# Routed experts of a one-core audio tower: groups of 384 rows in place of groups of 512

## What is computed

```python
h = _L0_tok_ref(x)                                  # 512 x 512 self attention over the channels of each batch
h = h + _L0_attn_ref(_layernorm(h), Wq, Wk, Wv, Wo) # 8 heads, 2 kv heads, 125 tokens a batch
h = h + _L0_ffn_ref(_layernorm(h), gate_w, w1, w2, w3, sw1, sw2, sw3, expert_bias)
```

```python
scores = softmax(xf @ gate_w)
_, sel = top_k(scores + expert_bias[None, :], 2)
routed_in = xf[token_idx] * top_scores_sorted[:, None]          # sorted by expert, 32000 rows of 512
h = silu(ragged_dot(routed_in, w1, counts)) * ragged_dot(routed_in, w3, counts)   # 512 -> 448
routed_out = ragged_dot(h, w2, counts)                          # 448 -> 512
out = (silu(xf @ sw1) * (xf @ sw3) @ sw2).at[token_idx].add(routed_out)
```

## Time and profile before

| | |
|---|---|
| median of 3 runs | 5948.72 us (5947.63 to 5953.92) |
| the profiled execution's own time | 5945.65 us |
| its span, first to last instruction | 5943.9 us |
| PE busy | 5809.3 us, 98% of the span |
| weight loads (PEld) busy | 4785.6 us, 81% |
| DVE busy | 4301.6 us, 72% |
| ACT busy | 2970.2 us, 50% |
| POOL busy | 2043.9 us, 34% |
| mean granted TensorE clock | 0.991 of 2.4 GHz |

### The profile page before, as it was taken

How to read it: one execution, slowest core, us unless ns; L and a number is a source line. 1 busy time by engine, 2 the same in 40 slices (tenths; PEclk the granted TensorE clock), 3 DMA queues, 4 the chain that set the end, 5 groups by cost and what they waited for, 6 DMA issues and landing times. The chain is left out here.

```text
span 5943.9 us, 103011 instructions
## 1 busy us (share of the span) xinstructions
PE 5809.3 (98%) x30600; PEld 4785.6 (81%) x30600; DVE 4301.6 (72%) x9758; ACT 2970.2 (50%) x5510; POOL 2043.9 (34%) x1725
## 2 busy tenths in 40 slices
PE   5999999999999999999999996999999999999999
PEld 4888888888888888888888885788888888888887
DVE  4888888888888888888888885666666666666665
ACT  3555555555555555555555553444444444444443
POOL 1333333333333333333333332333333333333332
PEclk8999999999999999999999998999999999999999
DMA  2111111111111111111111111666666556666641
GB/s 73 47 49 43 46 49 43 45 49 44 45 50 44 44 49 45 44 49 45 43 49 46 43 48 47 161 156 162 157 156 158 153 153 158 162 157 154 159 125 46
DMA packets 317180, 504.89 MB, mean 85 GB/s; under 512 B 78676, under 2 KB 151380, under 8 KB 317012
## 3 DMA queue, kind: packets, MB, share of 16 engines
q1 hardware_dynamic: 246228, 372.69, 20.8%
q0 software_dynamic: 70912, 131.71, 11.3%
HBM read 379.43 MB, written 140.28 MB: 87 GB/s over the span
## 5 line engine op out<-in xcount | busy, mean ns | idle before, releaser
L1428 POOL DMA_INDIRECT out_dram<-res,goal x280 | 530.6, 1895 | 1121.8 <-DMA out_dram<-res,goal 687.1
L930 POOL TENSOR_SCALAR ve<-ag 125x1 f32<-125x1 f32 x256 | 56.1, 219 | 1618.7 <-DVE ag L755 942.6
L639 ACT ACTIVATE e<-ps,negmax 128x512 f32<-128x512 f32 x512 | 349.2, 686 | 513.2 <-PE ps L449 408.0
L1172 PE MATMUL ps<-rT_hi,up_hi 128*128 128x512 f32 x1960 | 536.7, 395 | 1.6 <-DVE rT_lo L1336 1.6
L1172 PE MATMUL ps<-rT_lo,up_hi 128*128 128x512 f32 x1960 | 536.8, 395 | 0.0
L1172 PE MATMUL ps<-rT_hi,up_lo 128*128 128x512 f32 x1960 | 536.4, 395 | 0.0
L1264 ACT ACTIVATE uT_hi<-egb 128x512 fp32r<-128x512 f32 (+1 forms) x280 | 177.1, 632 | 540.4 <-DVE egb L1355 540.4
L1172 PEld LDWEIGHTS ps<-rT_hi,up_hi 128*128 128x128 f32 x1960 | 369.1, 188 | 89.9 <-issue 2.0
L1172 PEld LDWEIGHTS ps<-rT_lo,up_hi 128*128 128x128 f32 x1960 | 369.1, 188 | 88.0
L1172 PEld LDWEIGHTS ps<-rT_hi,up_lo 128*128 128x128 f32 x1960 | 368.9, 188 | 88.0
L942 POOL TENSOR_TENSOR qk_low<-X,qk_high 125x1024 fp32r<-125x1024 f32 x128 | 305.9, 2390 | 343.0 <-ACT qk_high L626 343.0
(11 more groups left out here) (216 smaller groups left out, 15487.4 us busy)
## 6 DMA issues: line engine op xcount, KB each, us to landing
raw<-in_L_ffn_w SPq DMA_DIRECT2D x140, 768.0 KB, 5.1
X<-in_x SPq DMA_DIRECT2D x128, 750.0 KB
raw<-in_L_ffn_w SPq DMA_DIRECT2D x70, 896.0 KB, 4.8
normed_rows<-y SPq DMA_DIRECT2D x128, 250.0 KB
out_dram<-h SPq DMA_DIRECT2D x128, 250.0 KB
raw<-in_L_ffn_w SPq DMA_DIRECT2D x210, 128.0 KB, 6.2
rows<-normed_rows,entries POOLq DMA_INDIRECT x280, 4.1
out_dram<-res,goal POOLq DMA_INDIRECT x280, 5.2
```

The costliest lines, as they stand in the source:

```text
L639: nc.scalar.activation(e[:, i, :], ps[:, (i + 1) % 2, :], ACT.Exp, bias=negmax[:, i:i + 1], accum_out=total[:, i:i + 1]).then_inc(e_sb.sem, 1)
L1172: ins = nc.tensor.matmul(ps[:, bank, :], w[a][:, k, col:col + P], rT[b][:, k, :], start=(k == 0 and i == 0), stop=(k == KC - 1 and i == 2))
L1428: nc.gpsimd.indirect_dma_start(out, bass.IndirectOffsetOnAxis(ap=goal[group[1] % 2][:, i:i + 1], axis=0), res[i][:], None, bounds_check=la ...
```

## The change

The number of tiles in a group goes from 4 to 3, and what follows from that: 91 groups (an odd number, so `each_group` has one more static call), planning that divides by three (five more small DVE operations), PSUM tiles cut to 384 columns in the up projection and the gate, signals of inner blocks counted by four (`block_of`) while those of tiles count by three, and waits for the tile that last used a bank (`LAST_IN_BANK`), since banks 0 and 1, and 6 and 7, no longer alternate evenly over groups. The four inner blocks of a group, its weights and their loads stay as they are.

```diff
-GROUP_TILES = 4
+GROUP_TILES = 3
...
     NG = (2 * TOKENS - E) // GROUP + E
-    NG += NG % 2
+    assert NG % 2 == 1
...
-                    then(nc.vector.tensor_scalar(groups[:], groups[:], float(GROUP - 1), None, ALU.add))
+                    then(nc.vector.tensor_scalar(groups[:], groups[:], float(P - 1), None, ALU.add))
                     then(nc.vector.tensor_copy(groups_i[:], groups[:]))
-                    then(nc.vector.tensor_scalar(groups_i[:], groups_i[:], GROUP.bit_length() - 1, None,
+                    then(nc.vector.tensor_scalar(groups_i[:], groups_i[:], P.bit_length() - 1, None,
                                                  ALU.logical_shift_right))
+                    then(nc.vector.tensor_copy(groups[:], groups_i[:]))
+
+                    then(nc.vector.tensor_scalar(groups[:], groups[:], float(GROUP_TILES - 1),
+                                                 float((1 << THIRD) // GROUP_TILES + 1), ALU.add, ALU.mult))
+                    then(nc.vector.tensor_copy(groups_i[:], groups[:]))
+                    then(nc.vector.tensor_scalar(groups_i[:], groups_i[:], THIRD, None, ALU.logical_shift_right))
                     then(nc.vector.tensor_copy(groups[:], groups_i[:]))
...
+            LAST_IN_BANK = (1, 3, 2)
...
-                with eng.Fori(1, NG // 2 - 1) as j:
+                with eng.Fori(1, (NG - 3) // 2) as j:
                     work((j, 0), False, 2)
                     work((j, 1), False, 2)
+                work((0, NG - 3), False, 2)
                 work((0, NG - 2), False, 1)
...
-                        pe.wait_ge(rT_lo.sem, rT_lo.at(back(t, 2)))
+                        pe.wait_ge(rT_lo.sem, rT_lo.at(back(t, LAST_IN_BANK[i])))
...
-                                ins = nc.tensor.matmul(ps[:, bank, :], w[a][:, k, col:col + P], rT[b][:, k, :],
+                                ins = nc.tensor.matmul(ps[:, bank, 0:GROUP], w[a][:, k, col:col + P], rT[b][:, k, :],
...
-                        pe.wait_ge(res_sb.sem, res_sb.at(back(t, 2)))
+                        pe.wait_ge(res_sb.sem, res_sb.at(back(t, LAST_IN_BANK[i])))
...
                         if left:
                             turn_rows(after, 2)
-                            turn_rows(after, 3)
-                        for i in (2, 3):
-                            down_full(group, i)
-                            down_tail(group, i)
+                        down_full(group, 2)
+                        down_tail(group, 2)
...
                         if left:
                             scale_rows(after, 2)
-                            scale_rows(after, 3)
...
                             rows_lo(after, 2)
-                            rows_lo(after, 3)
                         result(group, 2)
-                        result(group, 3)
...
                             gather(second, 2)
-                            gather(second, 3)
```

More of the change, by code:

```diff
@@ L987, in audio_tower @@
         group_expert = sbuf("group_expert", [1, NG], I32)
+        THIRD = 16
+        assert (TOKENS // P + GROUP_TILES) * ((1 << THIRD) // GROUP_TILES + 1) < 1 << 24
         with ExitStack() as c1:
@@ L1048, in audio_tower @@
             TAIL = HID - FULL * P
-            assert 2 * TAIL == P and T == FULL + 1
+            BLOCKS = FULL + 1
+            assert 2 * TAIL == P and T == 3
+            LAST_IN_BANK = (1, 3, 2)
             HALF = HID + TAIL
             raws = (sbuf("raw1", [P, KC, HID], F32, c2), sbuf("raw3", [P, KC, HID], F32, c2),
-                    sbuf("raw2", [P, T, D], F32, c2))
+                    sbuf("raw2", [P, BLOCKS, D], F32, c2))
             W13 = [[sbuf(f"up_{part}{p}", [P, KC, 2 * HID], F32R, c2) for part in ("hi", "lo")] for p in range(2)]
-            W2 = [[sbuf(f"down_{part}{p}", [P, T, D], F32R, c2) for part in ("hi", "lo")] for p in range(2)]
+            W2 = [[sbuf(f"down_{part}{p}", [P, BLOCKS, D], F32R, c2) for part in ("hi", "lo")] for p in range(2)]
             entries = pair("entries", [P, T, ENTRY])
@@ L1061, in audio_tower @@
             gb = pair("egb", [P, GROUP])
-            uT = [sbuf("uT_hi", [P, T, GROUP], F32R, c2), sbuf("uT_lo", [P, FULL, GROUP], F32R, c2)]
+            uT = [sbuf("uT_hi", [P, BLOCKS, GROUP], F32R, c2), sbuf("uT_lo", [P, FULL, GROUP], F32R, c2)]
             res = [sbuf(f"res{i}", [P, D], F32, c2) for i in range(T)]
@@ L1086, in tile_of, with block_of @@
                 return (T * j, T * off + i)
+            def block_of(group, c):
+                j, off = group
+                return (BLOCKS * j, BLOCKS * off + c)
             def landed(group):
@@ L1181, in down_full @@
                             pe.wait_ge(w_lo[2].sem, w_lo[2].at(group))
-                            pe.wait_ge(uT_hi.sem, uT_hi.at(tile_of(group, FULL - 1)))
-                        pe.wait_ge(res_sb.sem, res_sb.at(back(t, 2)))
+                            pe.wait_ge(uT_hi.sem, uT_hi.at(block_of(group, FULL - 1)))
+                        pe.wait_ge(res_sb.sem, res_sb.at(back(t, LAST_IN_BANK[i])))
                         for n, (a, b) in enumerate(PASSES):
                             if i == 0 and n == 2:
-                                pe.wait_ge(uT_lo.sem, uT_lo.at(tile_of(group, FULL - 1)))
+                                pe.wait_ge(uT_lo.sem, uT_lo.at(block_of(group, FULL - 1)))
                             for k in range(FULL):
@@ L1194, in down_tail @@
                         if i == 0:
-                            pe.wait_ge(uT_lo.sem, uT_lo.at(tile_of(group, FULL)))
+                            pe.wait_ge(uT_lo.sem, uT_lo.at(block_of(group, FULL)))
                         for b in range(2):
@@ L1211, in work @@
                         for c in range(FULL):
-                            pe.wait_ge(gb_sb.sem, gb_sb.at(back(tile_of(group, c), 2)))
+                            pe.wait_ge(gb_sb.sem, gb_sb.at(back(block_of(group, c), 2)))
                             up(group, 2 + 2 * (c % 2), c * P).then_inc(u_ps.sem, 1)
                             up(group, 3 + 2 * (c % 2), HALF + c * P).then_inc(u_ps.sem, 1)
-                        pe.wait_ge(gb_sb.sem, gb_sb.at(back(tile_of(group, FULL), 2)))
+                        pe.wait_ge(gb_sb.sem, gb_sb.at(back(block_of(group, FULL), 2)))
                         up(group, 4, FULL * P).then_inc(u_ps.sem, 2)
@@ L1235, in split_up @@
                         act.wait_ge(w_in[n].of(group), w_in[n].at(group))
-                        act.wait_ge(u_ps.sem, u_ps.at(tile_of(back(group, 2), T - 1)))
+                        act.wait_ge(u_ps.sem, u_ps.at(block_of(back(group, 2), FULL)))
                         nc.scalar.activation(W13[group[1] % 2][0][:, :, n * HID:(n + 1) * HID], raws[n][:],
@@ L1255, in tanh @@
                     def tanh(group, c, n=P):
-                        t = tile_of(group, c)
+                        t = block_of(group, c)
                         act.wait_ge(u_ps.sem, u_ps.at(t, 1))
                         act.wait_ge(ga_sb.sem, ga_sb.at(back(t, 1)))
-                        nc.scalar.activation(th[0:n, :], ps[0:n, 2 + 2 * (c % 2), :], ACT.Tanh,
+                        nc.scalar.activation(th[0:n, :], ps[0:n, 2 + 2 * (c % 2), 0:GROUP], ACT.Tanh,
                                              scale=0.5).then_inc(th_sb.sem, 1)
                     def inner_hi(group, c, n=P):
-                        act.wait_ge(gb_sb.sem, gb_sb.at(tile_of(group, c)))
+                        act.wait_ge(gb_sb.sem, gb_sb.at(block_of(group, c)))
                         nc.scalar.activation(uT[0][0:n, c, :], gb[c % 2][0:n, :], ACT.Copy).then_inc(uT_hi.sem, 1)
@@ L1291, in work @@
                         tanh(group, 3, TAIL)
-                        act.wait_ge(gb_sb.sem, gb_sb.at(back(tile_of(group, 3), T)))
-                        nc.scalar.activation(vb[0:TAIL, :], ps[TAIL:P, 4, :], ACT.Copy).then_inc(vb_sb.sem, 1)
+                        act.wait_ge(gb_sb.sem, gb_sb.at(back(block_of(group, FULL), BLOCKS)))
+                        nc.scalar.activation(vb[0:TAIL, :], ps[TAIL:P, 4, 0:GROUP], ACT.Copy).then_inc(vb_sb.sem, 1)
                         if left:
@@ L1300, in work @@
                             rows_hi(after, 2)
-                            rows_hi(after, 3)
                     each_group(act, work)
@@ L1344, in gate @@
                         dve.wait_ge(gb_sb.sem, gb_sb.at(back(t, 1)))
-                        nc.vector.scalar_tensor_tensor(ga[0:n, :], th[0:n, :], 1.0, ps[0:n, b, :],
+                        nc.vector.scalar_tensor_tensor(ga[0:n, :], th[0:n, :], 1.0, ps[0:n, b, 0:GROUP],
                                                        ALU.add, ALU.mult).then_inc(ga_sb.sem, 1)
@@ L1350, in gate @@
                             dve.wait_ge(u_ps.sem, u_ps.at(t))
-                            other = ps[:, b + 1, :]
+                            other = ps[:, b + 1, 0:GROUP]
                         else:
```

## The result

The changed kernel takes **5921.88 us** in the median of six runs (5920.18 to 5922.86), the kernel before 5948.18 us beside it (5946.8 to 5953.92): a ratio of 0.9956, 95% interval 0.9945 to 0.9966, **26 us faster**. The profiled execution took 5922.86 us with a span of 5921.1 us, against 5945.65 and 5943.9. The forecast was 5931 us in a range of 5906 to 5968.

The account below looks back on a forecast made before the run. PE's issue was taken as the bound: 14.78 up projection + 7.67 down + 1.31 transposes + 0.27 wait + 0.04 left over = 24.07 us a group; 91 groups take 2190.4 against 2208.2 us, -18, giving 5931 us, range 5906 to 5968.

Parts of the forecast that it names:

- PE's issue bounds the kernel: Expert loop: PE's matmuls and transposes set the pace, 31.50 us of a 31.55 us group before the change.
- The price at 384: Up projection: each 384-column matmul costs 176 ns, between 174.4 and 180; 7644 of them replace 5880 of 512 columns.
- The wait that appears: Before tile 2's down projection, PE waits for DVE's copy of tile 0: 0.27 us a group, bounds 0.13 and 0.37.
- The other waits cost nothing: Tile 2's low part (1.2 us of cover left) and the inner values do not hold PE; costed at nothing.
- The cover of block 2's high part: Inner values: block 2's high part ends about 1.0 us before the first down matmul needs it.
- The weight loads cost nothing: DMA in the loop: loads issued a good ten microseconds ahead of use cost nothing; share 70% in all.
- The scatter-adds: POOL's chain, each add waiting for the landing before: three take 21.5 us of the new 24.07 us group.
- The long interval of the prediction: Kernel before: of three start-to-start intervals between scatter-adds, 5.59, 9.99 and 5.91 us, the 9.99 us one.
- Rival 1: Tile 0's copy wait costs nothing and a 384-column matmul takes 174.4 ns: 5894 us; chance 0.06.
- Rival 2: Up projection: weight loads of 188 ns set the pace of 384-column matmuls, +92 us, 6023 us; chance 0.05.
- Rivals 3 and 4: 3: scatter-adds become the bound, 6043 us, chance 0.06. 4: block 2's high part comes late, 5977 us, chance 0.05.

Follow-up runs that it names:

- groups of 256: Against the changed kernel, two tiles a group instead of three, 132 groups of 256 rows: 6169.24 us, ratio 1.0373 to the kernel before.
- after_again: The changed kernel run again unaltered, on one chip beside the kernel before and follow-up kernels: 5922.57 us, ratio 0.9958.
- the early tail: Changed kernel with tile 0's last two down-projection matmuls issued ahead of tile 1's third pass: 5898.93 us, ratio 0.9921 to the kernel before.
- small loads: Kernel with 256-row groups, its loop loading only a quarter of w1 and w3 and a third of w2's first part: 6158.75 us, ratio 1.0357.
- the widths: Kernel before, with the loop's up-projection matmuls cut to 448, 384, 320 or 256 columns by product, work left out: 5711.61 us, single execution.
- less cover: Changed kernel with tile 2's row transposes for the next group moved ahead of the last matmuls of tiles 0 and 1: 5957.63 us, ratio 1.0019.

## Why the prediction was right

- *PE's issue bounds the kernel*: shown. The period without the wait is the sum of PE's prices to 0.01 us.
- *The price at 384*: 176 ns forecast, 176.0 measured. Of the readings named, the line through 256 and 512 (175) was the closest; the nanosecond put on top of it was a choice that no row backed, and that it fits so well is luck. The bounds of 174.4 and 180 ns were what made the range wide, and neither was reached.
- *The wait that appears*: right in place and kind, 0.27 us forecast, 0.21 measured. The rows gave 0.21; the 0.06 on top were for a slower release in the loop, and PE goes on 0.75 us after the copy's start in the loop too. That is 5 us of the total, and most of the distance between -18 and -24 us; period 24.07 against 24.00. The 2 us from -24 to the -26 of the medians lie within the scatter of the runs.
- *The other waits cost nothing*: right. The cover of block 2's high part was put at 1.0 us; it was a little less, as ACT's and PE's timelines show:

```profile
4602.62 0.53 ACT L1278 ACTIVATE uT_hi<-egb 128x384 fp32r<-128x384 f32 x1 [2.71 <-DVE egb L1367]
...
4603.94 0.94 PE L1204 MATMUL ps<-down_hi,uT_hi 128*128 128x512 f32 x3
```

  It ends at 4603.15, 0.79 us before the matmul that reads it, and it is what gives way in groups of 256.
- *The weight loads cost nothing*: right, share 72% for 70%.
- *The scatter-adds*: right that they are not the bound, but the account of their chain was too short. It put three adds at 21.5 us of 24.07. From start to start the first two take 5.80 and 7.30 us (means over the loop of after_again); the third lands 8.7 us after its start, and the other adds follow a landing by 0.87 us, which makes 9.5: some 22.6 us of the 24.00, an estimate. (The bracket of the third add below names a load of entries, but in after_again its start follows the second add's landing by 0.87 us as well.) The next add comes 10.9 us after the third only because it waits for DVE's result copy. So about 1.4 us a group are to spare where 2.6 were worked out, and with the early tail half of that is gone and the copies wait. The long interval of the prediction, 9.99 us, did not shrink; it moved from the second add to the third, with DVE's split:

```profile
4610.59 1.62 POOL L1438 DMA_INDIRECT out_dram<-res,goal  x1 [2.01 <-DVE res L1385]
...
4616.44 1.58 POOL L1438 DMA_INDIRECT out_dram<-res,goal  x1 [2.87 <-DMA out_dram<-res,goal]
...
4623.44 2.02 DVE L1333 TENSOR_TENSOR up_lo<-raw,up_hi 128x1792 fp32r<-128x1792 f32 x1
...
4623.61 3.29 POOL L1438 DMA_INDIRECT out_dram<-res,goal  x1 [5.58 <-DMA entries<-routed_entries]
...
4635.60 1.62 POOL L1438 DMA_INDIRECT out_dram<-res,goal  x1 [4.25 <-issue]
```

  There the add starts 0.17 us into the split. In another group it starts 0.02 us after the split's start and is not held:

```profile
5391.47 2.08 DVE L1333 TENSOR_TENSOR up_lo<-raw,up_hi 128x1792 fp32r<-128x1792 f32 x1
...
5391.49 1.58 POOL L1438 DMA_INDIRECT out_dram<-res,goal  x1 [5.45 <-DMA entries<-routed_entries]
```

  Of the 75 third adds between 4000 and 5800 us of this trace, 69 start 0.04 to 1.52 us into the split, and every one of them ends 1.44 to 1.46 us after the split's end, wherever in the split it started. The other six start before the split or within 0.03 us of its start, and take 1.6 us. In after_again the quick ones land 4.8 us after their start in the median, the held ones 8.7. So POOL's part of an add waits for the end of a subtraction on DVE that is under way. The landing is later by more than this wait, and the weight loads have a share in it: at 256 rows with small loads an add that is held just so is followed 7.4 us later, with full loads 9.8 us.
- *Rival 1* did not happen, the wait is there and the price is 176 ns; but the wait can be covered by an order, and the early tail shows the 5899 us that go with it. *Rival 2* is refuted by the widths. *Rivals 3 and 4* did not happen at 384; at 256 the runs fit both, together.

What the prediction did not say is how little of the gain is speed: without empty groups the two are 2 to 6 us apart.

## What to carry to other kernels

A tile size under a fixed bound on the number of groups has two effects of opposite sign: fewer tiles that the bound asks for, and a higher price per tile; work out both, and see which the inputs pay for. When a group gets shorter, look at each pair of "write, copy out, write again" on the bounding engine: the copy's latency stays, the cover shrinks, and reordering a few instructions can be worth as much as the change. When an experiment removes one limit and little happens, remove the next one with it before the theory is given up.

## What the runs showed of the hardware

An fp32r matmul against 128 loaded columns costs 118 to 120, 147, 176, 204 and 232.5 ns at 256, 320, 384, 448 and 512 moving columns at granted clock 1.00, though each load of weights is recorded for 188 ns: the records of the loads overlap the matmuls and each other. Refilling a PSUM bank behind DVE's 128x512 copy takes from the last matmul into that bank 1.27 us in the loop of "less cover", 1.29 in that of the changed kernel, and 1.18 in the last group of the kernel before. An indirect scatter-add that waits for the one before starts 5.8 to 10 us after it. The short end is an add that finds DVE free of a split, the long end one that starts during a split of 1536 to 1792 columns with the weight loads beside it; its part on POOL then ends 1.44 to 1.46 us after the split in the changed kernel, and is 1.6 us long otherwise.
